# A compressed interaction network on one core: a fifth unit through PSUM, halves one unit apart, a tenth unit on GpSimd, and new last rounds

## What is computed

```python
e = jnp.stack([tbl_f[ids[:, f]] for f in range(39)], axis=1)      # 1024 x 39 x 16
for i, (W, b) in enumerate(zip(Ws, bs)):                          # three layers, L = 128
    Wr = W.reshape(F0, Fk, L)
    z = jnp.einsum('bfd,bgd->bfgd', x, h)
    cur = jax.nn.relu(jnp.einsum('bfgd,fgl->bld', z, Wr) + b[None, :, None])
    # the first 64 of 128 maps are the next h, the others go to the output;
    # of the last layer all 128 go to the output
z = jnp.concatenate(outs, axis=1).sum(-1)
h = jnp.concatenate([z, dense_ctx], axis=1)
h = jnp.maximum(h @ W_top1 + b_top1, 0.0)
h = jnp.maximum(h @ W_top2 + b_top2, 0.0)
y = h @ W_top3
```

## Time and profile before

| what | value |
|---|---|
| median of 3 runs | 1286.15 us (1285.22 to 1287.26) |
| the profiled execution | 1286.31 us, its span 1284.2 us |
| PE busy | 1215.5 us, 95% of the span |
| DVE busy | 1113.8 us, 87% |
| POOL busy | 1036.5 us, 81% |
| ACT busy | 816.4 us, 64% |
| DMA | 156.17 MB, mean 122 GB/s |

### The profile page before, as it was taken

How to read it: one execution, slowest core, us unless ns; L and a number is a source line. 1 busy time by engine, 2 the same in 40 slices (tenths; PEclk the granted TensorE clock), 3 DMA queues, 4 the chain that set the end, 5 groups by cost and what they waited for, 6 DMA issues and landing times.

```text
span 1284.2 us, 14380 instructions
## 1 busy us (share of the span) xinstructions
PE 1215.5 (95%) x4180; PEld 767.5 (60%) x4180; DVE 1113.8 (87%) x1274; ACT 816.4 (64%) x1115; POOL 1036.5 (81%) x629
## 2 busy tenths in 40 slices
PE   0598999999999999999999999999999999999899
PEld 0254566666666666666666666666666666766545
DVE  2189999999999999999999999999999999999753
ACT  1147566666676667666676667666666778777553
POOL 7458888888988888888988888888988778888733
PEclk9999999999999999999999999999999999999999
DMA  8193466655555566655555666655455665654100
GB/s 185 24 230 93 108 143 147 146 134 116 111 125 119 132 146 147 146 130 115 112 123 122 135 146 147 147 123 118 113 117 123 139 144 144 142 119 118 33 1 1
DMA packets 102510, 156.17 MB, mean 122 GB/s; under 512 B 20811, under 2 KB 32988, under 8 KB 102322
## 3 DMA queue, kind: packets, MB, share of 16 engines
q1 hardware_dynamic: 92256, 152.56, 50.2%
q0 software_dynamic: 10176, 2.70, 2.1%
HBM read 151.31 MB, written 6.19 MB: 123 GB/s over the span
## 4 chain that ended last, share of the span: by engine, by line
PE 80%; DVE 7%; issue 4%; POOL 4%; ACT 4%; DMA 0%; another core or an unknown queue 0%; DVEq 0%; ACTq 0%; POOLq 0%
PE curM L987 36%; PE curM L1004 13%; PE curM L1012 13%; PE curM L1005 13%; DVE z L618 4%; POOL emb L348 3%; ACT h L850 2%; PE xk L976 2%; DVE zl L705 1%; ACT zh L816 1%; DVE zl L696 1%; POOL zl L359 1%; DVE curY L684 1%; DVE z L669 0%; PE h L1110 0%
## 5 line engine op out<-in xcount | busy, mean ns | idle before, releaser
L359 POOL TENSOR_TENSOR zl<-z,zh 128x1024 fp32r<-128x1024 f32 (+1 forms) x301 | 718.4, 2396 | 146.9 <-ACT zh L816 131.0
L618 DVE TENSOR_TENSOR z<-xr,h 128x1024 f32<-128x1024 f32 x456 | 548.4, 1212 | 3.8 <-issue 3.1
L987 PE MATMUL curM<-z,wf 128*128 128x512 f32 (+3 forms) x1220 | 537.4, 600 | 1.0 <-ACT h L850 0.9
L816 ACT ACTIVATE zh<-z 128x1024 fp32r<-128x1024 f32 (+1 forms) x320 | 337.8, 1056 | 291.1 <-DVE z L618 150.6
L348 POOL DMA_INDIRECT emb<-in_tbl_dram,idx x312 | 311.5, 998 | 89.7 <-issue 54.5
L1004 PE MATMUL curM<-zh,wl 128*128 128x512 f32 (+1 forms) x816 | 374.9, 459 | 4.8 <-issue 3.2
L987 PEld LDWEIGHTS curM<-z,wf 128*128 128x128 f32 (+3 forms) x1220 | 214.7, 188 | 237.6 <-issue 217.2
L1005 PE MATMUL curM<-zh,wh 128*128 128x512 f32 (+1 forms) x816 | 321.4, 394 | 0.0
L1012 PE MATMUL curM<-zl,wh 128*128 128x512 f32 (+1 forms) x816 | 255.5, 394 | 9.6 <-POOL zl L359 5.1
L850 ACT ACTIVATE h<-curM,bias 64x512 f32<-64x512 f32 x372 | 240.4, 646 | 20.0 <-DVE z L618 9.9
L696 DVE TENSOR_TENSOR zl<-curY,zh 128x512 fp32r<-128x512 f32 x240 | 164.9, 687 | 71.0 <-ACT zh L801 69.1
(11 more groups left out here) (140 smaller groups left out, 391.0 us busy)
## 6 DMA issues: line engine op xcount, KB each, us to landing
xr<-xT SPq DMA_DIRECT2D x384, 192.0 KB
xs<-xT SPq DMA_DIRECT2D x279, 156.0 KB
xq<-xT SPq DMA_DIRECT2D x64, 256.0 KB
emb<-in_tbl_dram,idx POOLq DMA_INDIRECT x312
xs<-xT SPq DMA_DIRECT2D x62, 78.0 KB
xT<-xc SPq DMA_DIRECT2D x31, 78.0 KB
xr<-in_L_rec_W_dram SPq DMA_DIRECT2D x16, 144.0 KB
xT<-xc SPq DMA_DIRECT2D x31, 40.0 KB
```

The costliest lines, as they stand in the source:

```text
L359: nc.gpsimd.tensor_tensor(zl[0:n, SNUM[r, u] % NL, :], z[0:n, z_slot(r, u), :], zh[0:n, SNUM[r, u] % NH, :], ALU.subtract).then_inc(lo_poo ...
L618: return nc.vector.tensor_tensor(z[:, slot, :].rearrange("p (a n) -> p a n", a=2), x, h, ALU.mult)
L816: nc.scalar.activation(zh[0:n, SNUM[r, u] % NH, :], z[0:n, z_slot(r, u), :], ACT.Copy).then_inc(hi_ready, 1)
L987: mm = nc.tensor.matmul(cur[:, :], wf[rows, full_at(u), a, :], z[rows, z_slot(r, u), a * N:(a + 1) * N], start=start and i == 0, stop=stop ...
```

## The change

- `KINDS`: unit 15 goes from F to P (D in rounds 0 and 31). There are five P units, 1, 6, 12, 15 and 17.
- `half_lag` is 1 in every round: a P unit's first half is subtracted, and its second half written, at the next unit; the second is subtracted at the one after that.
- `TENTH` = 4: unit 4 is G instead of F in rounds 3 to 24, save where r % 4 is 2 (17 rounds). Its weights are split in round 1 at unit 2 on ACT and POOL.
- Last rounds: units 8 and 19 are F again in rounds 29 and 30; the ReLUs of layer 1 of round 29 are spread over unit 18 of round 29 and units 0 to 2 of round 30.

```diff
--- before.py
+++ after.py
@@ -33,7 +33,7 @@
 
 
 
-KINDS = "GPGFFGPGFF" + "FGPGFFGPGF" + "FGFF"
+KINDS = "GPGFFGPGFF" + "FGPGFPGPGF" + "FGFF"
 UNITS = len(KINDS)
 A_END, C_END = 10, 20
 FIRST, LAST = -3, STEPS - 1
@@ -44,7 +44,11 @@
 LAST_AT, SPREAD_AT, COPY_AT = 1, 3, 7
 
 LATE_A, LATE_C = (3, 8), (14, 19)
-LATE = LATE_C + LATE_A
+
+TENTH = 4
+LATE = (TENTH,) + LATE_C + LATE_A
+
+SHORT, LONGER = (STEPS - 3, STEPS - 2), (8, 19)
 LATE_FROM = 25
 
 POOL_FROM = 11
@@ -59,6 +63,10 @@
 
 
 def kind(r, u):
+    if r in SHORT and u in LONGER:
+        return "F"
+    if u == TENTH and 3 <= r < LATE_FROM and r % 4 != 2:
+        return "G"
     if ((r >= LATE_FROM and u in LATE_C) or (r > LATE_FROM and u in LATE_A)):
         return "G"
 
@@ -100,7 +108,7 @@
 
 def half_lag(r):
 
-    return 1 if r == STEPS - 2 else 2
+    return 1
 
 
 def behind(r, u, halves):
@@ -384,8 +392,10 @@
                 for n, u in enumerate(spread):
                     if kind(r, u) == "G":
                         subtract(r, u)
-                    if r == LATE_FROM and 2 <= u < 2 + len(LATE):
-                        weight_lo_late(u - 2)
+                    if (r, u) == (1, 2):
+                        weight_lo_late(0)
+                    if r == LATE_FROM and 2 <= u < 1 + len(LATE):
+                        weight_lo_late(u - 1)
                     if gathers and r > 0 and n == 2 and part == 0:
                         pool.wait_ge(idx_loaded[b % 2], 16 * (b // 2))
                         pool.nop(nofuse=True)
@@ -898,8 +908,10 @@
                     if r == -2 and u == UNITS - 1:
                         for i in DIRECT_FIRST:
                             take0(r, i)
-                    if r == LATE_FROM and 2 <= u < 2 + len(LATE):
-                        weight_hi_late(u - 2)
+                    if (r, u) == (1, 2):
+                        weight_hi_late(0)
+                    if r == LATE_FROM and 2 <= u < 1 + len(LATE):
+                        weight_hi_late(u - 1)
                     if u == SPREAD_AT and r >= 1 and fresh(r) and r <= STEPS - 4:
                         copy_emb((r + 3) // PER_B)
                     if u == LAST_AT and r >= 1:
@@ -916,7 +928,12 @@
                     if 0 <= r <= STEPS - 4:
                         for i in {C_END - 2: [DIRECT], C_END: [0, 1, 2, 3], C_END + 1: [4, 5]}.get(u, []):
                             take1(r, i)
-                    if u == UNITS - 1 and (r == -1 or STEPS - 4 < r <= STEPS - 2):
+                    if r == STEPS - 3 and u == C_END - 2:
+                        take1(r, DIRECT)
+                    if r == STEPS - 2 and u < 3:
+                        for i in range(2 * u, 2 * u + 2):
+                            take1(r - 1, i)
+                    if u == UNITS - 1 and r in (-1, STEPS - 2):
                         for i in DIRECT_FIRST:
                             take1(r, i)
 
@@ -992,7 +1009,7 @@
                     w_low, w_high = wl, wh
                     if KINDS[u] == "F":
                         w, w_low, w_high = LATE.index(u), wl_late, wh_late
-                        if r <= LATE_FROM + 1:
+                        if r <= LATE_FROM + 1 and (u != TENTH or r < 6):
                             pe.wait_ge(w_hi, HI_OPS + w + 1)
                             pe.wait_ge(w_lo, LO_OPS + w + 1)
                     pe.wait_ge(hi_ready, SNUM[r, u] + 1)
```

## The result

The changed kernel takes 1465.69 us (median of 4, 1465.11 to 1467.23) against 1286.31 us (1285.22 to 1287.26) of the kernel before: ratio 1.1392, 95% interval 1.1376 to 1.1407. It is 13.9% slower. The forecast was 1462 us, and slower with a chance of 0.96.

A forecast was written before the change was run, and what follows sets the result against it. PE was taken to bound the kernel, with DVE's slack 2.3 us a round. Added DVE work and waits of 175.6 us on the profiled execution's 1286.3 gave 1462 us, range 1430 to 1490, or 1390 to 1492 reaching to a rival.

The forecast's parts named there:

- The bound moves from PE to DVE waiting for ACT: Usual rounds: DVE's round becomes 42.05 us, 6.3 us above PE's work, so PE's gain is worth nothing; chance 0.78.
- The waits: DVE's first-half subtractions: 1.16 us more at units 1 and 6, 0.84 at 15 and 17, 2.63 at 12; 6.75 a round.
- The round: Rounds 1 to 28: 33.9 us base, 1.4 work for unit 15 and 6.75 waits make 42.05 us, against 36.18.
- the base of 33.9 us: DVE's own work in a round of the kernel before, taken as 36.18 x 280.88/300 from busy time.
- "Costs nothing": the tenth unit: Unit 4 as G: 1.06 us of rounding on ACT, no P unit right behind; POOL's 2.4 us covered by slower rounds.
- The last rounds: Rounds 25 to 28: unit 14 is G, its rounding stands before unit 15's, +0.3 us each, 1.3 us in all.
- The ends: Rounds 0 and 31: unit 15 as D adds one line 705 instruction each, partly beside other work, +2.5 us.
- the sum: 164.4 us for rounds 1 to 28, 7.4 for round 29, 0 for round 30, 1.3 and 2.5: 175.6 us together.
- What would show it: After: some 190 us idle at line 696, rounds of 42 us, PE below 90% in the middle, chain over DVE and ACT.
- The clock: PE's new gaps might lower its clock; to bound again it needs a mean under 0.85. Within a rival of chance 0.11.
- the other case weighed: Shared GpSimd and DVE port: each of 17 POOL passes stops DVE 2.4 us, 41 us, 1503 us; within a rival of 0.11.

The follow-up runs named there:

- a product in front of each subtraction: Changed kernel with second halves written two units after the first, subtracted one unit later, and unit 18 P instead of 17: 1306.73 us, ratio 1.0198 to the kernel before.
- the kernel without the fifth unit: Changed kernel with unit 15 back as F and the old lag of 2 (1 in round 30): 1271.86 us, ratio 0.9928 to the kernel before; again 0.9930.

## Why the prediction was right, point by point

- **The bound moves from PE to DVE waiting for ACT.** Shown by the chain, and by the runs in both directions: the lag alone makes 9.0%, and a product in front of each subtraction takes 11.9 of 13.9% back.
- **The waits.** From half to subtraction I had 1.76, 1.76, 3.23, 1.44 and 1.44; measured 1.76, 1.76, 3.24, 1.43 and 1.43. Round 30 of the kernel before had held the price, and ACT's queue could be replayed from the earlier trace rows.
- **The round.** Predicted 42.05 us. Rounds 1 to 24 are 41.52, or 42.24 in the two of four that have an extra reduction, 41.88 on average without the tenth unit's delays: 0.17 too much, 4 us in 24 rounds. The waits fit to a hundredth, so what was too high is the base of 33.9 us that I took from busy time. An instruction in front of a wait counts there with its whole duration, a product with 1.21 us, and not with the 1.13 us from its start to the next one's. So the two waits of a round before are still partly in the base. From start to start, with these waits taken out, the trace before gives 33.8 us, and the changed one 41.88 - 1.40 - 6.75 = 33.7.
- **"Costs nothing": the tenth unit.** Wrong in five rounds, 0.64 us each, through the `zh` ring and PE's late start after ACT's copy. I had only looked for a P unit right behind unit 4, and had counted slots of time on ACT but not slots of the ring. My other sentence on it, that in a 36 us round POOL would be the bound with 38 us of work, was wrong too: the kernel without the fifth unit has tenth units in rounds of eleven gathers and keeps PE busy throughout. POOL's work has to fit over four rounds, not in each: its subtractions and gathers take 273.75 of 300 us there.
- **The last rounds.** The term that was mis-sized most. Rounds 25 to 28 were to cost 1.3 us more than the others; they are 43.1, 43.2, 44.8 and 43.9, 7.5 us more. I had counted unit 14's rounding in front of unit 15 only. Unit 12's half waits 2.97 us in rounds 26 to 28, because unit 8's rounding pushes the ReLUs of unit 10 back on ACT. Unit 15's waits 1.07 instead of 0.73. Unit 1's waits 2.00 from round 26 on; ACT at the end of round 28, from unit 19's rounding to unit 1's half:
```profile
1326.25 1.06 ACT L826 ACTIVATE zh<-z 128x1024 fp32r<-128x1024 f32 x1
1327.34 2.66 ACT L860 ACTIVATE h<-curM,bias 64x512 f32<-64x512 f32 x4
...
1331.01 1.32 ACT L860 ACTIVATE h<-curM,bias 32x512 f32<-32x512 f32 x2
1332.27 1.04 ACT L826 ACTIVATE zh<-z 128x1024 fp32r<-128x1024 f32 x1
1333.21 0.57 ACT L811 ACTIVATE zh<-curY 128x512 fp32r<-128x512 f32 x1
```
Unit 19 is F in a usual round. As G it puts 1.06 us in front of six ReLUs, which stand in front of unit 0's rounding, which starts 1 us after its product is written. Unit 6's half waits 1.93 us in round 27 (1.94 in round 29), where ACT stands still for PE to free a slot of `zh`: unit 3 is G there, as unit 4 is in the tenth unit's rounds. What the halves of units 6, 12, 15 and 1 wait beyond a usual round accounts for the longest of these rounds: 42.24 us and 0.86 + 0.43 + 0.34 + 0.93 are 44.8. So the step that failed is that late G units were counted only where a P unit stands right behind them. Round 29 is 39.7 us (37.8 predicted), round 30 38.9 (38.8, as before).
- **The ends.** I had 2.5 us for unit 15 as D in rounds 0 and 31 and measured 0.2 in all, but not since the term was right. Round 0 alone pays 3.4 us for it (46.9 against 43.5 us with the fifth unit taken out). The start-up was 1.4 us shorter this time, which the prediction had no term for; in the other runs on chips at 1286.7 us round 0's reduction starts at 107.9 to 109.0. So round 1's first product starts 3.4 - 1.4 = 2.0 us later. The stretch from round 30's last product to the end is 1.8 us shorter, by the new last rounds, for which I had 0. Two errors cancel here.
- Against the 175.6 us of the sum stand 179.3: rounds 1 to 28 +4.0 (the last ones +6.2, the tenth unit +3.2, the base the rest down), round 29 +1.9, the ends -2.3.
- **What would show it.** Idle before line 706 (696 before): 190 expected, 197.4 found. PE below 90% in the middle: 91% found. PE's work there is 35.5 of 41.9 us by the earlier trace rows, 85%; a matmul's record is longer than its distance to the next, so a busy time hides short gaps.
- **The clock** did not fall with PE's gaps: 1.00 in the middle. The rule of the Trainium skill (TensorE: Matmul & The Clock Gate, Part 1) that idleness lowers it did not come into play in that stretch. The 41 us of the other case weighed did not come either: taking the 17 passes on GpSimd away changed some 3 us, and the waits of ACT for PE account for them. The read port that GpSimd and DVE share by the Trainium skill (Perfetto Trace Analysis, Optimizing Scalar/DVE Operations) thus shows no cost in these rounds, where DVE has an input in PSUM.

## What to carry to other kernels

When a helper engine stands in the middle of a chain A, B, A, count what A has to do between its two steps: a full instruction there hides the helper, an empty place shows its whole duration, handoffs and whatever stands in its queue. Saving time on the engine that bounds is worth no more than the slack of the next one, here 2.3 us a round, and a change that shortens distances between steps spends slack without adding work. If some rounds of a kernel already run in the planned way, read the price there.

## What the runs showed of the hardware

Line 705 before, 715 after, subtracts with both inputs in SBUF. The earlier trace rows had 1.2 to 3.7 us for it. In round 0 of the changed kernel, with POOL subtracting at the same time, one took 5.65 us; DVE first, then POOL:
```profile
129.72 3.72 DVE L715 TENSOR_TENSOR zl<-z,zh 128x1024 fp32r<-128x1024 f32 x1
133.36 3.47 DVE L628 TENSOR_TENSOR z<-xr,h 128x1024 f32<-128x1024 f32 x3
136.76 5.65 DVE L715 TENSOR_TENSOR zl<-z,zh 128x1024 fp32r<-128x1024 f32 x1
...
144.60 1.21 DVE L715 TENSOR_TENSOR zl<-z,zh 128x1024 fp32r<-128x1024 f32 x1
...
129.98 2.37 POOL L367 TENSOR_TENSOR zl<-z,zh 128x1024 fp32r<-128x1024 f32 x1
...
134.29 7.03 POOL L367 TENSOR_TENSOR zl<-z,zh 128x1024 fp32r<-128x1024 f32 x3
```
The long one ends at 142.41, 1.09 us after POOL's third subtraction, that is about its own 1.2 us. The one at 144.60 has POOL idle and takes 1.21. The three products at 133.36, whose input h is in PSUM, keep their pace of 1.13 us while POOL subtracts, and the half subtractions, with one input in PSUM, stay between 679 and 694 ns through all 300. The bound of 3.7 us for line 705 was too low.

The kernel before took 1280.9 us on one chip and 1286.7 on two others. In the experiments the first reduction of round 0 starts at 103.1 to 103.5 us on the one and 107.9 to 109.0 on the others. The kernel without the fifth unit ran on two of them, and its rounds 1 to 29 took 1006.8 and 1007.0 us: the difference lies in the start-up, in which part of it was not looked into, and ratios have to be taken on one chip.
